# Who takes the low parts of the feed-forward weights, and when Pool adds the last attention residual's bias

## The reference, cut to what matters

```
for layer in (0, 1):
    x = x + tanh(g_xattn[layer]) * attention(layernorm(x), ctx)      # ctx_1024: 2 x 154 x 512
    h = layernorm(x) @ W1 + b1                                       # 512 -> 2048
    h = relu(h)                     if layer == 0
    h = piecewise_linear_gelu(h)    if layer == 1                    # on a grid of 1/256, 33 points
    x = x + tanh(g_ffn[layer]) * (h @ W2 + b2)                       # 2048 -> 512
```

## Time and profile before

| | before |
|---|---|
| median of 3 runs | 2540.95 us (2539.31 to 2540.98) |
| the profiled execution | 2540.6 us, of which the profile spans 2538.8 |
| mean granted TensorE clock | 0.987 |
| busy: TensorE, VectorE, ScalarE, Pool | 96%, 56%, 43%, 13% |
| TensorE's instructions of matmul | 12840 |

### The profile page before, as it was taken

One profiled execution on the slowest core, in us unless ns is written; L12 is line 12 of the kernel. 1 busy time (PEld: TensorE's weight loads), 2 busy tenths in 40 slices (PEclk: granted clock), 3 DMA queues, 4 the chain that ended last, 5 costly groups with the idle time before them and its releaser, 6 DMA issues.

```text
span 2538.8 us, 32081 instructions
## 1 busy us (share of the span) xinstructions
PE 2443.0 (96%) x12840; PEld 1844.0 (73%) x12864; DVE 1433.5 (56%) x2326; ACT 1081.4 (43%) x1754; POOL 324.2 (13%) x279
## 2 busy tenths in 40 slices
PE   7999999999999999999889999999889999999997
PEld 5666677688888888887655566665678888888885
DVE  5555665432222222223765555554689888888986
ACT  4444334432222222222343333334466666666664
POOL 1011112440000000000201111122420000000000
PEclk9999999999999999999999999999999999999999
DMA  3211113411101110121221111122400100101100
GB/s 123 67 51 50 51 51 115 137 59 44 50 17 34 50 50 8 43 73 56 70 77 31 64 64 64 64 67 88 149 17 34 50 17 34 51 17 50 34 34 17
DMA packets 87942, 140.92 MB, mean 56 GB/s; under 512 B 4849, under 2 KB 27761, under 8 KB 87793
## 3 DMA queue, kind: packets, MB, share of 16 engines
q1 hardware_dynamic: 87792, 138.87, 16.2%
HBM read 105.30 MB, written 33.55 MB: 55 GB/s over the span
## 4 chain that ended last, share of the span: by engine, by line
PE 41%; DVE 8%; ACT 2%; issue 1%; POOL 0%; DVEq 0%; ACTq 0%
PE l_lay_bank L69 18%; PE l_lay_score L69 12%; PE l_lay_score L1358 1%; PE l_lay_values L1429 1%; PE l_lay_score L1412 1%; PE l_lay_score L1360 1%; PE l_lay_score L1406 1%; DVE l_at_at_next L993 1%; PE l_lay_sums L1441 1%; PE l_lay_values L1433 1%; DVE l_at_full L989 1%; DVE l_at_at_next L1000 1%; DVE l_at_h_lo L1014 1%; DVE l_at_xTf_lo L895 1%; DVE l_at_maxes L942 1%
## 5 line engine op out<-in xcount | busy, mean ns | idle before, releaser
L69 PE MATMUL l_lay_score<-l_at_tw_hi,l_at_h_hi 128*128 128x512 f32 x1024 | 404.6, 395 | 15.3 <-DVE l_at_h_lo L1014 14.9
L69 PE MATMUL l_lay_score<-l_at_tw_hi,l_at_h_lo 128*128 128x512 f32 x1024 | 401.1, 392 | 0.0
L69 PE MATMUL l_lay_score<-l_at_tw_lo,l_at_h_hi 128*128 128x512 f32 x1024 | 401.0, 392 | 0.0
L69 PE MATMUL l_lay_bank<-l_at_xTf_hi,l_at_tw_hi 128*128 128x512 f32 x1024 | 400.3, 391 | 0.0
L69 PE MATMUL l_lay_bank<-l_at_xTf_lo,l_at_tw_hi 128*128 128x512 f32 x1024 | 398.6, 389 | 0.0
L69 PE MATMUL l_lay_bank<-l_at_xTf_hi,l_at_tw_lo 128*128 128x512 f32 x1024 | 398.5, 389 | 0.0
L974 DVE TENSOR_TENSOR l_at_h_lo<-l_at_full,l_at_h_hi 128x512 fp32r<-128x512 f32 x128 | 98.0, 766 | 472.0 <-ACT l_at_h_hi L722 472.0
L717 ACT ACTIVATE l_at_full<-l_lay_bank,l_at_lay_b 128x512 f32<-128x512 f32 x128 | 88.3, 690 | 457.8 <-PE l_lay_bank L69 457.8
L69 PEld LDWEIGHTS l_lay_score<-l_at_tw_hi,l_at_h_hi 128*128 128x128 f32 x1024 | 193.6, 189 | 61.2 <-DVE l_at_h_lo L1014 21.9
L69 PEld LDWEIGHTS l_lay_score<-l_at_tw_hi,l_at_h_lo 128*128 128x128 f32 x1024 | 193.7, 189 | 41.0
L69 PEld LDWEIGHTS l_lay_score<-l_at_tw_lo,l_at_h_hi 128*128 128x128 f32 x1024 | 193.8, 189 | 39.3
(11 more groups left out here) (218 smaller groups left out, 4181.7 us busy)
## 6 DMA issues: line engine op xcount, KB each, us to landing
both_x_in<-stream SPq DMA_DIRECT2D x25, 1024.0 KB, 5.6
l_at_xg<-stream SPq DMA_DIRECT2D x23, 1024.0 KB, 5.5
stream<-l_at_xg SPq DMA_DIRECT2D x22, 1024.0 KB, 4.3
l_at_tw_raw<-in_l_w SPq DMA_DIRECT2D x64, 256.0 KB, 5.9
both_x_in<-in_x SPq DMA_DIRECT2D x9, 1024.0 KB, 7.5
out<-l_at_xg SPq DMA_DIRECT2D x8, 1024.0 KB, 4.3
l_at_xg<-in_x SPq DMA_DIRECT2D x7, 1024.0 KB, 5.4
l_at_maskT_in<-in_maskT SPq DMA_DIRECT2D x8, 512.0 KB, 4.4
```

The lines of the kernel that those rows point to most:

```text
L69: done = nc.tensor.matmul(out, lhs[a], rhs[b], start=first and n == 0, stop=last and n == len(passes) - 1)
```

## The change

Both layers run the same code, so each edit acts twice.

First, VectorE gets a function of its own for the low parts, `weights_lo_late`, with a semaphore of its own; Pool keeps tiles 0 and 1 only. VectorE makes tiles 2 to 5 ahead of the four steps of `y_back(last)`, and tile m+4 in step m of the first feed-forward chunk. Pool's list is left with the six copies of `widen` in a row.

Second, in the last attention chunk Pool does `add_bias(last)` right behind `add_bias(last - 1)`, ahead of the second half of `widen(last - 1)`.

```diff
-        w_hi, w_lo = n.sem("w_hi"), n.sem("w_lo")
+        w_hi, w_lo, w_lo_late = n.sem("w_hi"), n.sem("w_lo"), n.sem("w_lo_late")
...
                 if it:
                     widen(it - 1, range(RB))
                     add_bias(it - 1, gate_bias)
+                if it == last:
+                    add_bias(last, gate_bias)
                 if norm and it < last:
                     q_rstd_of(it + 1)
                 if it < last:
                     x_rstd_of(it + 2)
                 if it:
                     widen(it - 1, range(RB, KT))
-                if it == last:
-                    add_bias(last, gate_bias)
                 if it == last - 1:
                     weights_lo(0)
                     weights_lo(1)
-            widen(last, range(RB))
-            weights_lo(2)
-            weights_lo(3)
-            widen(last, range(RB, KT))
-            for m in range(2, MT):
-                for mm in ((4, 5, 6) if m == 2 else (m + 4,)):
-                    if mm < MT:
-                        weights_lo(mm)
-                if m == 8:
-                    x_rstd_of(NCH + 1)
+            widen(last, range(KT))
+            x_rstd_of(NCH + 1)
...
+            def weights_lo_late(m):
+                for i in range(2):
+                    dve.wait_ge(w_hi, 2 * m + i + 1)
+                    nc.vector.tensor_tensor(tw_lo[m][:, i, :], tw_raw[m][:, i, :],
+                                            tw_hi[m][:, i, :].bitcast(F32), ALU.subtract)\
+                        .then_inc(w_lo_late, 1)
...
             for q in range(QT):
+                weights_lo_late(2 + q)
                 y_back(last, q)
             for u in range(2, MT * NCH):
                 f, m = u // MT, u % MT
...
+                if f == 0 and m + 4 < MT:
+                    weights_lo_late(m + 4)
                 if f < last or ahead:
                     if m == 7:
                         norm_stats(NCH + f + 1)
...
             def first_product(u):
                 f, m = u // MT, u % MT
                 if f == 0:
-                    pe.wait_ge(w_lo, 2 * m + 2)
+                    if m < 2:
+                        pe.wait_ge(w_lo, 2 * m + 2)
+                    else:
+                        pe.wait_ge(w_lo_late, 2 * m - 2)
```

## The result

The changed kernel takes 2513.51 us, the median of 4 runs (2512.85 to 2514.2), against 2540.97 us before (4 runs, 2539.31 to 2541.17): a ratio of 0.9892, with a 95% interval of 0.9879 to 0.9904. It is 27.5 us faster; the forecast was 2512.8. The profiled execution spans 2512.4 us at a mean granted clock of 0.991, against 2538.8 and 0.987.

The account below looks back on a forecast made before the run. TensorE is nearly always busy, losing time to waits for VectorE, which Pool's work stretches. Gains of 4.4 (first layer), 8.4 (second layer's turn) and 15.3 (feed-forward chunk) sum to 28.1 us, giving 2512.8; 8-in-10 range 2507.5 to 2520.

Parts of the forecast that it names:

- First layer: Turn from attention to feed-forward: moving the bias removes a 2.74 us TensorE wait and 1.71 of slow clock, 4.4 us.
- Second layer's turn: Attention to feed-forward: 28.4 us hold 19.0 of TensorE work; about 1.0 of waiting stays, so 8.4 us gained.
- The chunk: Second layer's first feed-forward chunk: VectorE's step falls from 7.17 to 5.25 us, under TensorE's 5.45; gain 15.3 us.
- the wait behind the statistics: In that feed-forward chunk, TensorE waits 1.9 us for h_lo(6), ready at 35.5 and wanted at 33.6.
- the 1.7 us charged for a fall: Extra TensorE time in that feed-forward chunk, for the clock falling after a wait of 1.9 us.
- another wait, of 1.1 at tile 9: TensorE's next wait in that feed-forward chunk, 1.1 us, taken to be hidden by the earlier delay.
- Only the difference of prices: Rival, feed-forward stage: moving a pair saves only 1.25 us a tile, step 5.9, total 2516.6; chance 0.14.
- the chunk gives nothing: Rival: h_lo stays as late in the feed-forward stage, only bias and turn pay; 2528 us, chance 0.05.
- the slower case: Rival: VectorE's pair waits for ScalarE's high part, held by the weights' DMA; 2553 us at 4 us a step, chance 0.04.
- More than forecast: Rival, feed-forward stage: clock stays up through a wait of 1.9 us and the statistics cost less; 2509 us, chance 0.07.
- The signs named in advance: Changed profile: Pool's add at 447 and about 1737 to 1741, L956 pairs of 1.3, step 5.25 to 5.45, h_lo waits 5 or 6.
- the prediction's line between 1.45 (up) and 2.38 (down): TensorE's clock in the feed-forward chunk: stayed up through a 1.45 us wait, fell after 2.38; 1.9 was judged nearer the latter.

Follow-up runs that it names:

- run 3: Changed kernel plus, in the second layer, 28 Pool subtractions at the old places whose result nobody uses; 2529.15 us, ratio 0.9951 to the kernel before.
- run 4: Changed kernel plus, in the second layer, useless Pool memsets, five a step, which write the same scratch tile and read nothing; 2514.73 us.
- Run 2: Changed kernel with the last bias put back behind the second half of the widening, VectorE keeping the low parts; 2521.64 us.
- run 5: Changed kernel, but in the first layer Pool makes the low parts of tiles 2 to 15 as before; 2514.13 us.
- Run 7: Changed kernel, but in the second layer's first feed-forward chunk statistics move from m = 7 to 11, normalising from 10 to 13; 2512.95 us.
- run 8: Changed kernel, but in the second layer nobody makes low parts of tiles 2 to 15; TensorE reads the high parts instead; 2509.96 us.
- run 6: Changed kernel, but in the second layer each VectorE low-part subtraction is followed by a useless one of the same size; 2525.86 us.

## Why the prediction was right, and where a size was off

**What bounds the kernel.** Right. Pool, which no row of TensorE's waits names, was the cause: run 3 brings 15.6 us back with Pool instructions that have no tie of data to what they delay, and run 4, which leaves Pool as busy, brings 1.2 in the medians, within their scatter, and 0.6 in the chunk.

**First layer, 4.4 forecast, 4.3 measured.** Run 2 (34.03) shows that all of it is the bias, run 5 that the low parts give nothing there. The side effects priced at zero were zero: the add now lies on another VectorE instruction that nobody needs soon (L973, two of them, 9.53 us together under the two adds, from 443.63), and TensorE doesn't feel it.

**Second layer's turn, 8.4 forecast, 8.5 measured.** From the first projection (1756.93) to that of the last chunk (1776.94) TensorE takes 20.0 us, as the sum said (28.4 - 8.4). The second tile's GELUs run at 0.68, and the last wait is 0.59 where "about 1.0" was put. The two copies of Pool do still stretch two of VectorE's operations, to 1.09 and 0.91 us.

**The chunk, 15.3 forecast, 15.2 measured; the mechanism was right, but that the two numbers are so close is luck.** The step was put at 5.25 and is 5.19. From the first product of tile 2 (1787.82) the starts of tiles 4 to 8 were put at 10.3, 15.6, 20.9, 26.1 and 34.2, and are 10.25, 15.44, 20.62, 25.82 and 33.81. So the wait behind the statistics is 1.49 and not 1.9, and behind it the clock stayed up: the 1.7 us charged for a fall were not paid. By these two alone L981 of tile 15 would have come at 71.1 - 0.4 - 1.7 = 69.0.

It came at 70.29. The prediction had seen another wait, of 1.1 at tile 9, and put it at nothing, because the delay before would hide it. That delay was 2.1 us smaller, and the step with the normalising took VectorE 7.01 us (from 44.17 to 51.18), so the wait came: 0.78 us, at 1840.40. The rest is in small pieces: TensorE ends the product of tile 15 at 1857.78, which is 69.96, with 2.87 us of waits and 67.1 of work where 66.3 was put. L981 follows 0.3 us later, with no idle time ahead of it: VectorE's own list and TensorE arrive within tenths of each other there. To this point the gain is 86.4 - 70.3 = 16.1 us, 0.8 more than forecast.

The sum ended there, and the stretch measured here goes on to the head of the next chunk, where 1.0 us is lost again: from tile 15 to 16 are 10.49 us against 9.52 before. Before, VectorE had no idle time in between, since its L982 of tile 15 had waited for TensorE and ScalarE's part was done by then; now it waits once for ScalarE:

```profile
1859.74 0.69 DVE L1013 SCALAR_TENSOR_TENSOR l_at_h_lo<-l_at_at_grid,l_at_h_hi 128x512 fp32r<-128x512 f32 x1 [0.89 <-ACT l_at_h_hi L740]
```

So what was missing in the working is VectorE's list from the statistics to the end of the stage. I followed TensorE's sum there, and in the changed kernel VectorE has no wait for TensorE at all from 1794 to 1869. Run 7 agrees: without the wait behind the statistics the chunk gains 1.0, not the 3.6 us (1.9 + 1.7) that it was priced at.

**The rivals.** *Only the difference of prices* (step 5.9) falls: the step is 5.19, because the 0.88 us of idle time could be filled; run 8 has it back, and run 6 shows that from there on each 0.6 us more is paid in full in the step. That the chunk gives nothing falls too, and so does the slower case: no row of VectorE's L967 shows a wait for ScalarE's high part in the chunk. *More than forecast* fails although the clock stayed up (through a wait of 1.49 us), since the wait at tile 9 and the end of the chunk took that back. The Trainium skill's warning (Perfetto Trace Analysis, Optimizing Scalar/DVE Operations), that offloading between VectorE and Pool might not help, names the right cause, but in this direction the move gave 19.9 us (run 2): the Pool form of the pair blocked VectorE for more (7.17 - 5.19 = 2.0 us a step) than the own form costs it.

**The signs named in advance.** Pool's add at 447.59 and 1736.49, pairs of 1.29, 56 new VectorE instructions, a step of 5.19 (5.25 to 5.45 was said) and 6.1 us of waits for h_lo (5 or 6): as forecast or close to it. The longest wait, 1.90 us, stands at the end of the kernel and not behind the statistics.

## What to carry to other kernels

A Pool instruction that reads SBUF costs VectorE most of its own length when it meets an instruction with two SBUF inputs (here 3.6 us of a 4.6 us add, 0.85 us of a subtraction of 1.36), and the trace shows it as a long VectorE instruction and never as a wait: look for VectorE instructions far above their usual length that lie over one of Pool's. Work of this kind belongs on Pool only where VectorE has slack; where VectorE leads, give it the work outright, or move Pool's into a stretch in which VectorE idles. When the leader is lightened, follow both engines' lists to the end of the stage, since the next one may be only tenths behind.

## What the runs showed of the hardware

The last wait of TensorE, in front of the last hidden tile, is the same in all ten traces: 1.90 to 1.95 us, for the same h_lo. The granted clock of the 4.4 us behind it is 1.00 in five of them (before, runs 2, 3, 4 and 6) and 0.61 to 0.65 in the other five. Here TensorE's row in the changed kernel and the windows' row for it, and then the same two of the kernel before:

```profile
2494.02 0.61 PE L69 MATMUL l_lay_score<-l_at_tw_hi,l_at_h_hi 128*128 128x512 f32 x1 [1.90 <-DVE l_at_h_lo L1013]
...
2494.02:2498.42 4.40, 4.40 (x12) 3.30 (x12) 0.00 (x0) 0.00 (x0) 0.00 (x0) 0.61 0.00 0
```

```profile
2522.03 0.50 PE L69 MATMUL l_lay_score<-l_at_tw_hi,l_at_h_hi 128*128 128x512 f32 x1 [1.93 <-DVE l_at_h_lo L1014]
...
2522.03:2526.43 4.40, 3.01 (x12) 2.17 (x12) 1.29 (x3) 0.00 (x0) 0.00 (x0) 1.00 0.00 0
```

The same 12 matmuls take 4.6 us in one (up to 2498.64) and 3.0 in the other (up to 2525.04). That is the 1.6 us by which the two spans (26.4) differ less than the stretches (28.0). The length of a wait alone doesn't decide it, either: in run 6 the clock is 1.00 behind the wait of 2.15 us and 0.50 behind that of 3.42, by its windows' rows:

```profile
1801.41:1805.81 4.40, 4.40 (x19) 3.67 (x20) 4.26 (x8) 3.10 (x6) 0.00 (x0) 1.00 0.60 187
1829.77:1834.17 4.40, 4.40 (x10) 3.47 (x11) 4.26 (x8) 3.10 (x6) 0.09 (x1) 0.50 0.02 4
```

So the prediction's line between 1.45 (up) and 2.38 (down) can't be drawn: 1.9 fell five times and held five times. What decides stays open. No experiment was made on it.
